# Eight fp32 products of a zeroed tile on TensorE around the two modulation products of a transformer block

## The chip, the core and the metric

The kernel runs on one core of one Trainium2 chip. Its time is the device time of one execution in microseconds (us); lower is better. The engines are named as in the profile: PE is TensorE's matmul (PEld its weight load), DVE is VectorE, ACT is ScalarE, POOL is GpSimd, SP is SyncE, which issues most DMAs.

## What is computed

One conditioned transformer block on x of 32 sequences x 32 tokens x 256, all in fp32: an RMS norm whose scale comes from a product of the conditioning vector with a 256 x 256 matrix, attention with 8 query heads and one key and value head of 32 columns with rotary positions, a residual, a second RMS norm with a scale of its own, and a gated MLP of 1024.

```python
def ada_rms(x, t, w, tw):
    n = x * jax.lax.rsqrt(jnp.mean(jnp.square(x), axis=-1, keepdims=True) + EPS)
    scale = t @ tw.T
    return n * (w * (1.0 + scale))[:, None, :]
h = ada_rms(x, time_emb, ln1_w, ln1_tw)
q, k, v = heads(h @ Wq.T), heads(h @ Wk.T), heads(h @ Wv.T)
q = apply_rope(q, pos_ids)
k = apply_rope(k, pos_ids)
scores = jnp.einsum('bkgsd,bktd->bkgst', qg, k) / jnp.sqrt(jnp.float32(HD))
attn = jax.nn.softmax(scores, axis=-1)
x = res + ctx @ Wo.T
h = ada_rms(x, time_emb, ln2_w, ln2_tw)
mlp = jax.nn.silu(h @ Wg.T) * (h @ Wu.T) @ Wd.T
return res + mlp
```

(`heads` stands here for the reshapes.)

## The kernel before

The 1024 tokens are eight tiles of 128, taken two at a time as four groups, g = 0 to 3. Each engine has a program of its own, written out by hand in the order in which the engine runs it, and the programs meet only at semaphores. So the order on PE is that of the calls at the end of its block, and a product that PE has not yet come to holds up everything behind it.

PE begins with `norm_scale(0)` (L274 in the profile: four products of 128x32 into the bank `ps_s`, once `pa`, the pack with the conditioning and the first matrix, has landed). DVE turns them into the modulation `mod` (L454) and multiplies it into the transposed input, `hx` (L251). ACT rounds that to `hx_h` (L805), DVE or POOL takes the remainder `hx_l` (L256), and `qkv` (L293) forms the projections from three rounded products (high by high, low by high, high by low). The weights are split in the same way: `wqkv_h` on ACT (L868, L870) and `wqkv_l` on POOL (L977). Before the second tile's attention PE does `norm_scale(1)` (L274 into `ps_t`, once `pb` has landed), the modulation of the second norm. Then the first attention follows tile by tile: `scores` (L305), the maxima `top` (L574) and differences `below` (L583) on DVE, the exponential on ACT, `turn_probs` (L316), `context` (L330) and `project` (L340). All products that are not of the rounded kind, L274, L305, L330 and L340 among them, are plain fp32: each of them is two MATMULs in the trace. The rotation of queries and keys on DVE (`rot_b` L526, `rot_a` L533, `qkT` L556, `kbd` L562) needs tables that are made from the norm's factor.

From some 31 us on PE runs the gate and up products of the MLP (`gate_up`, L367) of one group, with the attention of the next group and the down products (L262 to L264) between them. The down products accumulate in two banks, of which `ps_d` is one; before that `ps_d` holds the projections of `qkv(1, 0)`, `qkv(2, 0)` and `qkv(3, 0)`, each of which begins by overwriting it.

Of the kernel before, what the change touches and what calls it, by code (L numbers as in the profile page):

```python
# [14 lines left out]
P = 128  # L15
BATCH, SEQ, HIDDEN = 32, 32, 256
# [39 lines left out]
def block_program(nc, xT, x_tok, pos, pack_s, pack_a, w_qkv, pack_b, w_gu, w_d, out):  # L56
    with ExitStack() as ctx:
        def sb(name, shape, dt=F32):
            return ctx.enter_context(nc.sbuf_tensor(name, shape, dt))

        def sem(name):
            return ctx.enter_context(nc.semaphore(name))
# [32 lines left out]
        sin = sb("sin", [P, 2, TILES, HALF])  # L95
        mod = [sb(f"mod{n}", [P, KH, BATCH]) for n in range(2)]
        half_neg = sb("half_neg", [P, CT])


        hx = sb("hx", [P, GROUPS, KH, GT])  # L100
# [39 lines left out]
        ps_d = ctx.enter_context(nc.psum_tensor("ps_d", [P, CT, HIDDEN], F32))  # L140
# [8 lines left out]
        out_done = sem("out_done")  # L149

        chain = sem("chain")
        half_ready = sem("half_ready")
        sin_ready = sem("sin_ready")
        mod_ps = sem("mod_ps")
        mod_ready = [sem(f"mod_ready{n}") for n in range(2)]
# [57 lines left out]
        def done(g, c, n):  # L213
            return g * CT + c + n

        def span(c, n, width):
            return slice(c * width, (c + n) * width)


        def bank_s(g, c, n):  # L220
            return ps_gu[:, 0].rearrange("p u t -> p (u t)") if (g, c) == (0, 1) else ps_s[:, :]
# [10 lines left out]
        def bank_qkv(g, c):  # L232

            if g == 0:
                return ps_a[:, c, 0:QKV]
            return (ps_d[:, :, :].rearrange("p c n -> p (c n)"),
                    ps_gu[:, RING - 1].rearrange("p u t -> p (u t)"))[c][:, 0:QKV]
# [29 lines left out]
        def _(pe):  # L267
            def norm_scale(n):

                w, loaded, bank = ((tw1, in_pa, ps_s), (tw2, in_pb, ps_t))[n]  # L270
                pe.wait_ge(loaded, 16)
                for f in range(KH):
                    for k in range(KH):
                        mm = pe.matmul(bank[:, span(f, 1, BATCH)], w[:, k, span(f, 1, P)], cond[:, k, :],  # L274
                                       start=(k == 0), stop=(k == KH - 1))
                mm.then_inc(mod_ps, 1)

            def qkv(g, c):


                if g > 1:
                    pe.wait_ge(qkv_copied, CT * (g - 2) + c + 1)
                maker, before = (0, 0) if g == 0 else (1, CT)
                pe.wait_ge(hx_hi, done(g, c, 1))
                for step, (x, w) in enumerate(((hx_h, wqkv_h), (hx_l, wqkv_h), (hx_h, wqkv_l))):
                    if step == 1:
                        pe.wait_ge(hx_lo[maker], done(g, c, 1) - before)
                    for k in range(KH):
                        if g == 0 and step == 0:
                            pe.wait_ge(wqkv_hi, k + 1)  # L290
                        if g == 0 and step == 2:
                            pe.wait_ge(wqkv_lo, k + 1)
                        mm = pe.matmul(bank_qkv(g, c), x[:, g, k, span(c, 1, P)], w[:, k, :],  # L293
                                       start=(step == 0 and k == 0), stop=(step == 2 and k == KH - 1))
                mm.then_inc(qkv_ready, 1)

            def scores(g, c0, n):
                if g == 0:
                    pe.wait_ge(mod_ready[0], 1)
                else:  # L300
                    pe.wait_ge(x2_ready, CT * g)
                pe.wait_ge(kbd_ready, done(g, c0, n))
                for c in range(c0, c0 + n):
                    for j in range(HG):
                        mm = pe.matmul(bank_s(g, c0, n)[:, span(c * HG + j, 1, P)], qkT[:, c, span(j, 1, P)],  # L305
                                       kbd[:, c].rearrange("p b t -> p (b t)"), start=True, stop=True)
                mm.then_inc(scores_ready, n)
# [75 lines left out]
                    mm.then_inc(down_ready, 1)  # L383


            norm_scale(0)
            qkv(0, 0)
            qkv(0, 1)
            norm_scale(1)
            scores(0, 0, 1)  # L390
            qkv(1, 0)
            turn_probs(0, 0, 1)
# [46 lines left out]
        def _(dve):  # L439
            steps = [0]  # L440

            def link(ins):
# [2 lines left out]
                ins.then_inc(chain, 1)  # L445
                dve.wait_ge(chain, steps[0])

            dve.memset(half_neg[:, :], -0.5).then_inc(half_ready, 1)

            def modulation():  # L450
# [598 lines left out]
```

## Time and profile before

| | us |
|---|---|
| three timed runs | 122.69, 124.89, 126.38 |
| median | 124.89 |
| span of the profiled execution, first to last instruction | 121.7 |
| PE busy in it | 104.9 (86%) |
| DVE busy | 86.7 (71%) |
| POOL busy | 53.5 |
| ACT busy | 53.0 |

Of the profiled execution only the span is recorded, not a device time of its own around it. The fastest timed run is 1.0 us above the span and the median 3.2 us. The three runs lie 3.7 us apart. In the timeline each row gives the start in us, the duration in us of all its instructions together, engine, line, operation, what is written and read, the shapes, the count, and in brackets the idle time of the engine before the row with what ended it. The durations of MATMULs overlap, so where one follows another the distance of their starts is the time that one takes.

### The profile page before, as it was taken

Reading aid. Unit: us, or ns where it says so; the run is one execution under the profiler, and the core shown is the slowest. Engines: PE = TensorE matmul, PEld = TensorE weight load, DVE = VectorE, ACT = ScalarE, POOL = GpSimd, SP = SyncE. Lnnn points to the kernel's source line nnn. Section 1 sums busy time; section 2 is a strip of 40 time slices with the busy share of each in tenths; the row PEclk is TensorE's granted clock in tenths of the full one; section 3 lists DMA queues with packets and bytes.
Section 4 is the critical chain, followed back from the end, with each engine's and each line's share of the span. In section 5 each row is a group of like instructions: output and inputs, shape, how many; then the busy total and the mean of one; then the engine's idle time right before and its main releaser. Section 6 shows DMA issues by size and latency. Waiting matters only on the chain.

```text
span 121.7 us, 2393 instructions
## 1 busy us (share of the span) xinstructions
PE 104.9 (86%) x768; PEld 100.5 (83%) x768; DVE 86.7 (71%) x207; ACT 53.0 (44%) x140; POOL 53.5 (44%) x59
## 2 busy tenths in 40 slices
PE   0658487983977999979999999999999999999991
PEld 0548366863867999969999999999999999999990
DVE  0587985789999976986889598688947453756411
ACT  4083578651951493143137624224562422455300
POOL 0065787756399429734033543402344231244610
PEclk9999869999687699999999999999999999999999
DMA  3999995000000000000000200000020000020011
GB/s 93 241 296 416 424 422 229 7 3 0 5 0 0 0 3 0 5 0 0 0 5 0 86 3 0 5 0 0 0 86 5 0 3 0 16 78 0 3 37 54
DMA packets 3421, 7.69 MB, mean 63 GB/s; under 512 B 592, under 2 KB 1616, under 8 KB 3408
## 3 DMA queue, kind: packets, MB, share of 16 engines
q1 hardware_dynamic: 3120, 7.25, 16.3%
q10 hardware_dynamic: 288, 0.27, 1.1%
q8 instruction: 7, 0.11, 0.4%
q14 instruction: 6, 0.05, 0.2%
HBM read 6.47 MB, written 1.05 MB: 62 GB/s over the span
## 4 chain that ended last, share of the span: by engine, by line
PE 63%; DVE 19%; issue 6%; DMA 4%; ACT 3%; POOL 1%; SPq 1%; DVEq 0%; POOLq 0%
PE ps_gu L367 34%; DVE kbd L562 4%; DMA wqkv<-in_w_qkv 4%; PE ps_s L305 4%; PE ps_a L264 3%; PE ps_a L262 3%; PE ps_a L263 3%; PE ps_d L262 3%; PE ps_d L263 3%; PE ps_d L264 3%; PE ps_a L330 2%; DVE rot_b L526 2%; DVE qkT L556 1%; PE ps_t L340 1%; PE ps_s L340 1%
## 5 line engine op out<-in xcount | busy, mean ns | idle before, releaser
L953 POOL TENSOR_TENSOR hf_l<-hf,hf_h 128x256 fp32r<-128x256 f32 x32 | 24.3, 758 | 45.5 <-ACT hf_h L853 45.5
L367 PE MATMUL ps_gu<-h_h,wgu_h 128*128 128x256 f32 x128 | 28.1, 302 | 0.2 <-ACT h_h L825 0.2
L367 PE MATMUL ps_gu<-h_h,wgu_l 128*128 128x256 f32 x128 | 26.6, 291 | 0.0
L367 PE MATMUL ps_gu<-h_l,wgu_h 128*128 128x256 f32 x128 | 26.6, 290 | 0.0
L846 ACT ACTIVATE th<-ps_gu 128x256 f32<-128x256 f32 x32 | 12.2, 382 | 24.9 <-PE ps_gu L367 24.8
L853 ACT ACTIVATE hf_h<-hf 128x256 fp32r<-128x256 f32 x32 | 13.2, 412 | 20.0 <-DVE hf L657 20.0
L367 PEld LDWEIGHTS ps_gu<-h_h,wgu_h 128*128 128x128 f32 x128 | 21.0, 200 | 0.6 <-ACT h_h L825 0.4
L648 DVE SCALAR_TENSOR_TENSOR sg<-th,ps_gu 128x256 f32<-128x256 f32 x32 | 13.3, 417 | 11.2 <-ACT th L846 10.8
L367 PEld LDWEIGHTS ps_gu<-h_l,wgu_h 128*128 128x128 f32 x128 | 20.8, 199 | 0.0
L367 PEld LDWEIGHTS ps_gu<-h_h,wgu_l 128*128 128x128 f32 x128 | 20.7, 199 | 0.0
L657 DVE TENSOR_TENSOR hf<-sg,ps_gu 128x256 f32<-128x256 f32 x32 | 13.4, 418 | 0.8
L966 POOL TENSOR_TENSOR wgu_l<-wgu,wgu_h 128x1024 fp32r<-128x1024 f32 x4 | 9.5, 2388 | 4.3 <-ACT wgu_h L857 4.3
L262 PE MATMUL ps_d<-wd_h,hf_h 128*128 128x256 f32 x32 | 9.1, 286 | 0.9 <-POOL hf_l L953 0.9
L262 PE MATMUL ps_a<-wd_h,hf_h 128*128 128x256 f32 x32 | 9.3, 290 | 0.0
L263 PE MATMUL ps_d<-wd_l,hf_h 128*128 128x256 f32 x32 | 9.1, 283 | 0.0
L264 PE MATMUL ps_a<-wd_h,hf_l 128*128 128x256 f32 x32 | 9.0, 282 | 0.0
L263 PE MATMUL ps_a<-wd_l,hf_h 128*128 128x256 f32 x32 | 9.0, 281 | 0.0
L264 PE MATMUL ps_d<-wd_h,hf_l 128*128 128x256 f32 x32 | 9.0, 281 | 0.0
L305 PE MATMUL ps_s<-kbd,qkT 128*128 128x128 f32 x28 | 4.7, 316 | 3.6 <-DVE kbd L562 3.6
L305 PEld LDWEIGHTS ps_s<-kbd,qkT 128*128 128x128 f32 x28 | 4.0, 218 | 3.8 <-issue 3.8
L262 PEld LDWEIGHTS ps_d<-wd_h,hf_h 128*128 128x128 f32 x32 | 6.0, 188 | 1.2 <-issue 1.1
L562 DVE TENSOR_TENSOR kbd<-qkT,small 128x128 f32<-128x128 f32 (+1 forms) x6 | 6.2, 1038 | 0.3
(117 smaller groups left out, 208.4 us busy)
## 6 DMA issues: line engine op xcount, KB each, us to landing
wgu<-in_w_gu SPq DMA_DIRECT2D x4, 512.0 KB, 10.4
wd<-in_w_d SPq DMA_DIRECT2D x2, 512.0 KB, 12.6
xk<-in_x_tok SPq DMA_DIRECT2D x1, 768.0 KB, 10.1
out_x<-xk SPq DMA_DIRECT2D x3, 256.0 KB, 2.2
pb<-in_pack_b SPq DMA_DIRECT2D x1, 576.0 KB, 8.5
xt<-in_xT SPq DMA_DIRECT2D x1, 512.0 KB, 9.2
wqkv<-in_w_qkv SPq DMA_DIRECT2D x1, 320.0 KB, 5.0
pa<-in_pack_a SPq DMA_DIRECT2D x1, 288.0 KB, 3.1
```

The costliest lines, as they stand in the source:

```text
L262: pe.matmul(ps, lhs_h, rhs_h, start=first, stop=False)
L263: pe.matmul(ps, lhs_h, rhs_l, start=False, stop=False)
L264: return pe.matmul(ps, lhs_l, rhs_h, start=False, stop=last)
L305: mm = pe.matmul(bank_s(g, c0, n)[:, span(c * HG + j, 1, P)], qkT[:, c, span(j, 1, P)], kbd[:, c].rearrange("p b t -> p (b t)"), start=Tru ...
L367: mm = pe.matmul(ps_gu[:, n % RING, part, :], w[:, m, span(part * KH + k, 1, P)], h[:, k, :], start=(step == 0 and k == 0), stop=(step == ...
L562: dve.tensor_tensor(kbd[:, cs, :, :], qkT[:, cs, HEADS * HD:QK].unsqueeze(2).broadcast_to([P, n, BPT, SEQ]), mask.unsqueeze(1).unsqueeze(3 ...
L648: dve.scalar_tensor_tensor(out=sg[:, n % RING], in0=th[:, n % RING], scalar=1.0, in1=ps_gu[:, n % RING, 0, :], op0=ALU.add, op1=ALU.mult). ...
L657: dve.tensor_tensor(hf[:, m], sg[:, n % RING], ps_gu[:, n % RING, 1, :], ALU.mult).then_inc(hf_ready, 1)
L846: act.activation(th[:, n % RING], ps_gu[:, n % RING, 0, :], ACT.Tanh, scale=0.5).then_inc(th_ready, 1)
L853: act.activation(hf_h[:, m], hf[:, m], ACT.Copy).then_inc(hf_hi, 1)
L953: pool.tensor_tensor(hf_l[:, m], hf[:, m], hf_h[:, m].bitcast(F32), ALU.subtract).then_inc(hf_lo, 1)
L966: pool.tensor_tensor(wgu_l[:, sl, :], wgu[:, sl, :], wgu_h[:, sl, :].bitcast(F32), ALU.subtract).then_inc(wgu_lo, 1)
```

## The change

A tile `blank` of 128 x 256 is set to zero by DVE as its first instruction. A new semaphore, `blank_ready`, is waited for by PE ahead of its first product. PE then multiplies `blank` with itself, 128 weight columns by 256 moving columns in plain fp32, into the first half of `ps_d`: four products ahead of `norm_scale(0)`, two behind it and two behind `norm_scale(1)`. Each product starts a sum of its own, and nothing reads the result; `qkv(1, 0)` overwrites the bank later. No other engine waits for these products.

```diff
+        blank = sb("blank", [P, HIDDEN])
...
+            def warm(n):
+
+                for _ in range(n):
+                    pe.matmul(ps_d[:, 0, :], blank[:, 0:P], blank[:, :], start=True, stop=True)
+
+            pe.wait_ge(blank_ready, 1)
+            warm(4)
             norm_scale(0)
+            warm(2)
             qkv(0, 0)
             qkv(0, 1)
             norm_scale(1)
+            warm(2)
             scores(0, 0, 1)
...
+            dve.memset(blank[:, :], 0.0).then_inc(blank_ready, 1)
             dve.memset(half_neg[:, :], -0.5).then_inc(half_ready, 1)
```

The start of PE's program before (a row's count is of products, not of MATMULs):

```order
0 L266 UNCONDITIONAL_BRANCH
1 L274 MATMUL ps_s<-pa 128x32 x4
2 L293 MATMUL ps_a<-wqkv_h,hx_h 128x320 x2
3 L293 MATMUL ps_a<-wqkv_h,hx_l 128x320 x2
4 L293 MATMUL ps_a<-wqkv_l,hx_h 128x320 x2
5 L293 MATMUL ps_a<-wqkv_h,hx_h 128x320 x2
6 L293 MATMUL ps_a<-wqkv_h,hx_l 128x320 x2
7 L293 MATMUL ps_a<-wqkv_l,hx_h 128x320 x2
8 L274 MATMUL ps_t<-pa,pb 128x32 x4
9 L305 MATMUL ps_s<-kbd,qkT 128x128 x2
```

The same stretch of PE's program now, where the new lines push the line numbers on by one (L390 is the new product):

```order
0 L267 UNCONDITIONAL_BRANCH
1 L390 MATMUL ps_d<-blank 128x256 x4
2 L275 MATMUL ps_s<-pa 128x32 x4
3 L390 MATMUL ps_d<-blank 128x256 x2
4 L294 MATMUL ps_a<-wqkv_h,hx_h 128x320 x2
...
9 L294 MATMUL ps_a<-wqkv_l,hx_h 128x320 x2
10 L275 MATMUL ps_t<-pa,pb 128x32 x4
11 L390 MATMUL ps_d<-blank 128x256 x2
12 L306 MATMUL ps_s<-kbd,qkT 128x128 x2
```

The three groups of new products stand ahead of the first modulation, between it and the first projection, and between the second modulation and the first scores; nothing else moved.

The start of DVE's program now:

```order
1 L458 MEMSET blank 128x256
2 L459 MEMSET half_neg 128x2
3 L493 TENSOR_TENSOR ang<-pos_sb,small 128x128
4 L495 TENSOR_SCALAR redu<-ang 128x128
5 L496 TENSOR_SCALAR turns<-redu 128x128
```

Only the first row is new; the others follow as before.

## Rows read from the trace of the kernel before

**Rows 1.** The page: chain that ended last, by engine and by line.

```profile
PE 63%; DVE 19%; issue 6%; DMA 4%; ACT 3%; POOL 1%; SPq 1%; DVEq 0%; POOLq 0%
PE ps_gu L367 34%; DVE kbd L562 4%; DMA wqkv<-in_w_qkv 4%; PE ps_s L305 4%; PE ps_a L264 3%; PE ps_a L262 3%; PE ps_a L263 3%; PE ps_d L262 3%; PE ps_d L263 3%; PE ps_d L264 3%; PE ps_a L330 2%; DVE rot_b L526 2%; DVE qkT L556 1%; PE ps_t L340 1%; PE ps_s L340 1%
```

**Rows 2.** Timeline, 0 to 12 us: first modulation, first projections, second modulation.

```profile
0.80 0.06 DVE L448 MEMSET half_neg<- 128x2 f32 x1 [0.80 <-PEq L1038]
...
3.86 1.92 PE L274 MATMUL ps_s<-pa 128*128 128x32 f32 x8 [3.86 <-DMA pa<-in_pack_a]
...
5.95 0.41 DVE L454 TENSOR_SCALAR mod<-ps_s,small 128x32 f32<-128x32 f32 x2
6.39 0.76 DVE L251 TENSOR_TENSOR hx<-xt,mod 128x256 f32<-128x256 f32 x2
6.71 0.47 ACT L868 ACTIVATE wqkv_h<-wqkv 128x320 fp32r<-128x320 f32 x1 [0.25 <-DMA wqkv<-in_w_qkv]
...
7.08 0.40 ACT L805 ACTIVATE hx_h<-hx 128x256 fp32r<-128x256 f32 x1
7.26 1.86 POOL L977 TENSOR_TENSOR wqkv_l<-wqkv,wqkv_h 128x320 fp32r<-128x320 f32 x2 [6.82 <-ACT wqkv_h L868]
...
7.54 0.99 PE L293 MATMUL ps_a<-wqkv_h,hx_h 128*128 128x320 f32 x2 [1.76 <-ACT hx_h L805]
...
8.32 0.95 DVE L476 SCALAR_TENSOR_TENSOR redu<-sin_in 128x128 f32<-128x128 f32 x1
...
11.56 1.08 PE L274 MATMUL ps_t<-pa,pb 128*128 128x32 f32 x8 [0.33 <-DMA pb<-in_pack_b]
...
11.83 0.52 DVE L526 TENSOR_TENSOR rot_b<-ps_a,sin_r 128x144 f32<-128x144 f32 x2
```

**Rows 3.** Timeline, 14 to 19 us: scores of the first and the second tile.

```profile
14.41 1.19 PE L305 MATMUL ps_s<-kbd,qkT 128*128 128x128 f32 x4 [1.77 <-DVE kbd L562]
...
15.63 0.42 DVE L574 TENSOR_REDUCE top<-ps_s 128x8 f32<-128x256 f32 x1 [0.58 <-PE ps_s L305]
...
17.02 0.69 PE L316 MATMUL ps_t<-pb,prob 128*128 128x128 f32 x2
...
18.14 0.68 PE L305 MATMUL ps_gu<-kbd,qkT 128*128 128x128 f32 x4 [0.43 <-DVE kbd L562]
```

**Rows 4.** Short stretches: busy per engine, granted clock, DMA share, GB/s.

```profile
14.10:14.20 0.10, 0.00 (x0) 0.00 (x0) 0.10 (x2) 0.00 (x0) 0.10 (x2) 0.94 1.03 430
14.20:14.30 0.10, 0.00 (x0) 0.00 (x0) 0.10 (x2) 0.09 (x1) 0.10 (x1) 0.50 1.23 512
17.50:17.60 0.10, 0.10 (x2) 0.00 (x0) 0.10 (x2) 0.10 (x1) 0.10 (x1) 0.50 0.90 369
17.60:17.70 0.10, 0.10 (x1) 0.00 (x0) 0.10 (x2) 0.07 (x1) 0.10 (x1) 1.00 0.99 410
```

**Rows 5.** Longer stretches; busy of PE, PEld, DVE, ACT, POOL; clock; DMA.

```profile
10.78:14.19 3.41, 1.52 (x11) 1.15 (x10) 3.27 (x10) 1.27 (x3) 2.00 (x3) 1.00 1.02 420
14.19:17.60 3.41, 3.19 (x12) 2.71 (x12) 2.76 (x10) 2.70 (x4) 3.41 (x3) 0.50 1.02 420
17.60:21.01 3.41, 2.57 (x17) 1.99 (x16) 2.29 (x8) 2.92 (x7) 2.10 (x2) 1.00 0.69 280
...
27.84:31.25 3.41, 1.60 (x10) 1.33 (x11) 3.29 (x6) 0.75 (x3) 1.44 (x1) 1.00 0.02 5
...
34.66:38.07 3.41, 1.62 (x14) 1.44 (x14) 3.38 (x5) 1.33 (x2) 3.41 (x3) 1.00 0.00 0
38.07:41.48 3.41, 3.41 (x19) 3.41 (x18) 3.35 (x5) 0.89 (x3) 2.21 (x3) 0.50 0.00 0
41.48:44.89 3.41, 3.41 (x31) 3.41 (x31) 2.58 (x7) 2.79 (x10) 1.38 (x2) 1.00 0.01 2
```

**Rows 6.** Timeline of PE, 49 to 51 us: projections of 128x256 in fp32.

```profile
49.75 1.02 PE L340 MATMUL ps_s<-pb,ctxT 128*128 128x256 f32 x4
50.61 1.03 PE L340 MATMUL ps_t<-pb,ctxT 128*128 128x256 f32 x4
```

More of the change, by code:

```diff
@@ L151, in block_program @@
         chain = sem("chain")
-        half_ready = sem("half_ready")
+        half_ready, blank_ready = sem("half_ready"), sem("blank_ready")
         sin_ready = sem("sin_ready")
```

## The prediction

> **What bounds the kernel now.** I read the chain of waits by engine first, to see who sets the end, then the timeline of the first 19 us, where the change lies, and last the granted clock in stretches. By the chain PE makes 63% of the span, and over half of that is the gate and up products [rows 1], which start at 31 us. The change touches nothing there. What it can do to the end is to bring the first attention, and with it everything behind it, earlier or later. So the question is what sets the pace from 0 to 19 us. In the timeline PE stands still until `pa` lands at 3.86, then again until 7.54, and waits 1.77 us before the scores at 14.41 and 0.43 us before those at 18.14 [rows 2, 3]: in that part it is mostly waiting for DVE, and a faster PE gains only where somebody waits for it. The one place of size is DVE's maximum at 15.63, which stood idle 0.58 us for the first scores [rows 3].
>
> The clock is the other reading. The granted clock falls to 0.50 (1.2 GHz) at 14.2 us and is back at 1.00 (2.4 GHz) at 17.6 [rows 4]. Before its first change the record says 1.00, but the durations do not bear it out: the eight MATMULs of the first modulation took 1.92 us, the same eight of the second 1.08 us [rows 2]. I take it that PE ran at the low level from the start until it had worked through the first projections. Behind each fall PE had been little busy: 1.52, 1.60 and 1.62 us in the 3.41 us ahead of 14.19, 31.25 and 38.07; in the stretch from 17.60, after which it kept 1.00, it was busy 2.57 us [rows 5].
>
> **The price of one product.** Two fp32 products of 128x256 are four MATMULs, and from the first of one set to the first of the next it is 50.61 - 49.75 = 0.86 us, so 0.43 us a product at 2.4 GHz [rows 6]. No row has them at 1.2 GHz. The scores went from 0.68 to 1.19 us between the levels [rows 3], a factor of 1.75, and twice is the most: 0.75 to 0.86 us a product, of which I take 0.86, since nothing but the array works on 256 columns.
>
> **The memset and the four products ahead of the first modulation.** The memset takes DVE's first place at 0.80 us. The trace has a memset of 128x2 with 0.06 us and an operation of 128x256 with 0.38 us (0.76 for two) [rows 2]: 0.06 to 0.38, and I take 0.3, near the upper end since the size is the same. On DVE it costs nothing, whose next work comes behind the DMA of the positions after 4 us. PE starts at 1.15 us and, at the low level, works 4 x 0.86 = 3.44 us, until 4.6. `pa` is there at 3.86, so the modulation starts 0.74 us later. If it also stays slow it ends at 6.5 and not at 5.78; DVE, which was ready for it only at 5.95, writes `mod` some 0.6 us later. From there: `hx` at 7.0, its first half done at 7.4, where ACT wanted it at 7.08, so 0.3 us late. The next cover is POOL: `wqkv_l` runs to 7.26 + 1.86 = 9.12 whatever `hx` does, and DVE's `redu` at 8.32 took 0.95 us although `hx`, twice as large, took 0.38 a piece, so it was held until POOL was through. The 0.3 us go into that stall, and the path to the tables and `rot_b` at 11.83 stays, or slips by up to 0.15 us by ACT's second half of `wqkv_h`, which stands behind `hx_h` in its queue. If the clock comes up within the four products, the modulation takes 1.08 us in place of 1.92 and even this is gone (4.3 + 1.1 = 5.4, before 5.78). I take 0 for this part, and -0.1 to +0.7 as bounds: the upper end is the whole delay without cover.
>
> **The two products behind it.** They stand before the first projection, which waits for `hx_h` until 7.54 [rows 2]. From 5.4 they end at 6.3 at the high level, from 6.5 at 8.2 at the low one. The second delays the first projection by 0.7 us. Its reader is `rot_b` at 11.83, which waits for the tables, and the two projections were through before the second modulation at 11.56 in spite of the low level; at the high level they would be done earlier. So 0 on the path; only `norm_scale(1)`, which waits for `pb` until 11.56, would start up to 0.3 us later.
>
> **The two products behind the second modulation.** It begins at 11.56 and ends at 12.64 at the high level. Two products end at 13.5, or at 14.35 if they are slow. The scores wait for `kbd` until 14.41 [rows 3], so both fit, the slow ones just. What they do is to fill the gap that stood before the fall at 14.19: PE's busy time there goes from 1.52 to 1.52 + 0.86 = 2.38 us. That is nearer to the 2.57 us of the stretch after which it kept the clock than to 1.62 us [rows 5]. If it is kept, the first scores take 0.68 us and not 1.19: 0.51 us earlier, less than the 0.58 us for which DVE idled, so DVE passes all of it on. `turn_probs` at 17.02 goes from 0.69 to some 0.69 / 1.75 = 0.4, on ACT's side, with nobody waiting who is on the path. The projections between them are hidden behind POOL's `hx_l` and DVE. So **-0.51 us**.
>
> **What is late next, and whether it lasts.** Behind the scores DVE, ACT and POOL follow one another by semaphores, and no DMA landing stands in the way: the DMA share is 1.02 up to 17.60, 0.69 to 21.01 and 0.00 from 27.84 [rows 5]. The chain shifts as a whole to the first group of the loop, where PE takes over. I find no place that gives it back for certain.
>
> **The sum.** 0 + 0 - 0.51 = -0.5 us, against the profiled execution 121.7 - 0.5 = 121.2 us of span. The same step on the median is 124.89 - 0.5 = **124.4 us**. The profiled execution lies 3.2 us under the median, and the three runs are 3.7 us apart, so the clock or something else differs from run to run by more than the whole gain. Within 2%, which is 2.5 us, a measurement of this kernel tells little from no change.
>
> The Trainium skill, page "TensorE: Matmul & The Clock Gate", Part 1, says that the default state is the throttled one and activity releases it, and adds for modelling that "the ramp penalty is <1% of a typical kernel span". By that rule no warm-up can give over 1.2 us here; my rows price it at 0.5, which agrees. The same page's table of what to do says that the clock falls back after an idle gap between bursts. This trace fell at 14.19 with 1.52 us of work before it, and no gap of PE there is over 1.8 us; the row decides.
>
> **The rivals.**
>
> First, **nothing arrives** (124.9 us): the clock is no better at 14.2 us, since the projections at the high level are themselves shorter, and PE, which then waits for POOL's `wqkv_l`, is less busy from 7.5 to 10.8. Then it falls before the second modulation, the last two products run slow and end at 13.5 + 1.7 = 15.2 us at worst, in front of the scores. Against a scores start of 14.41 this is +0.8 us, from which a clock that comes up meanwhile gives back 0.5 or more. For it: the low level is where PE's work fills its time. Against: 2.4 us of work in place of 1.5.
>
> Second, the one on the **slower side**: the fall is put off, not removed. With fast scores and projections PE is less busy between 14.2 and 17.6 than the 3.19 us that it had at the low level [rows 5]: 0.68 for the scores, 1.6 / 1.75 = 0.9 for what filled 15.4 to 17.02, and 0.4, some 2.0 us of work. If it falls at 17.6, the second tile is slow up to 21 us: scores +0.51, turning the probabilities +0.3, and the context products, which are four MATMULs of nearly the scores' size, +0.5, all on the chain: +1.3 - 0.5 = +0.8, so 125.7 us. It decides if those 2.0 us of work act like the 1.6 us ahead of a fall and not like the 2.57 us of the stretch that kept its clock; they lie halfway, and here a run of the clock's changes at other moments can turn it. It is slower, yet not by 2%; it would need another low stretch in the loop beside it, +1.3 us (below), to reach 127.4.
>
> Third, **more than the scores**: with the chain 0.5 us earlier, PE arrives earlier at the loop too and the fall at 38.07 does not come. In the low stretch from there PE did 19 MATMULs, in the next one of the same length 31 [rows 5], and it was on the path: 3.41 x (1 - 19/31) = 1.3 us. The time would be 124.4 - 1.3 = 123.1 us. For more than 2% a further 0.7 us would be needed, as from a run whose first attention was slow throughout.
>
> Fourth, **the first modulation's delay has no cover**: +0.7 - 0.5 = +0.2, 125.1 us.
>
> **How the numbers follow.** The forecast has 0.42; nothing arrives 0.22; put off 0.12; more than the scores 0.14; delay without cover 0.10. All of these lie between 123.1 and 125.7. The median itself moves by about 0.9 us with the luck of the runs (half of the mean distance from 124.89 to its neighbours, 1.5 and 2.2 us), which gives 122.2 to 126.6; since the upper cases hold less chance I end it at 126.2. Faster by over 2% (under 122.4) takes the third rival and luck: 0.11. Slower by over 2% (over 127.4) takes the second and bad luck: 0.06. Within 2%: 0.83.
>
> **What would show it.** In the profile of the changed kernel: PE's new products begin at about 1.15 us and take 3.0 to 3.5 us; the first modulation's eight MATMULs take 1.1 us and not 1.9; `redu` still ends at about 9.3 us and `rot_b` still starts at about 11.8; the granted clock is 1.00 at 14.4 and the first scores take about 0.7 us; DVE's maximum starts at about 15.1. I am wrong if `rot_b` starts over 0.3 us later, if the clock shows 0.50 between 14 and 21 us, or if the end moves by more than the start of the loop does.

## The result

| | executions | median us | lowest to highest |
|---|---|---|---|
| changed kernel | 4 | 124.66 | 124.37 to 127.39 |
| kernel before, the same session | 4 | 125.63 | 122.69 to 127.26 |

The ratio of the changed kernel to the one before was given as 1.019, 95% interval 1.0126 to 1.0253: slower, although its median is the lower one. The ratio counts only executions within 1.5% of the fastest of their kernel, which of these eight leaves the one of 122.69 us against three with a mean of 124.56 us, or 1.015, so the 1.019 cannot be worked out from them. The profiled execution of the changed kernel has a span of 122.6 us, 0.9 more than before, and took 124.37 us as a whole.

Later sessions ran both kernels again. Over all of them the changed kernel has 22 executions with a mean of 124.6 us (standard deviation 1.7) and the kernel before 76 with a mean of 124.8 us (1.7; two of 254 and 257 us left out). The difference is -0.1 us with a standard error of 0.4; with each of the three sessions that ran both compared by itself it is -0.5 +- 0.5 us. So **the eight products made no difference that could be measured**. The forecast of -0.5 us lies within the error, and so does zero; the 0.9 us more of the first comparison of spans lies over two errors away, so I take the first ratio for chance.

The page of the changed kernel, chain by engine and by line:

```profile
PE 68%; DVE 17%; issue 6%; DMA 3%; ACT 3%; POOL 0%; SPq 0%; DVEq 0%
PE ps_gu L368 33%; DVE kbd L573 4%; PE ps_s L306 4%; PE ps_a L294 3%; DMA pos_sb<-in_pos 3%; PE ps_a L264 3%; PE ps_a L265 3%; PE ps_a L263 3%; PE ps_d L263 3%; PE ps_d L264 3%; PE ps_d L265 3%; PE ps_a L331 2%; PE ps_d L390 2%; PE ps_s L341 1%; PE ps_t L341 1%
```

Against [rows 1] the first link is another: the chain starts at the DMA of the positions, `pos_sb`, and no longer at the weights, and the new products (L390) hold 2% of it. The timeline of the same stretch as [rows 2] and [rows 3]:

```profile
0.86 0.27 DVE L458 MEMSET blank<- 128x256 f32 x1 [0.86 <-PEq L1049]
...
1.19 3.66 PE L390 MATMUL ps_d<-blank 128*128 128x256 f32 x8 [1.19 <-DVE blank L458]
...
4.68 0.97 PE L275 MATMUL ps_s<-pa 128*128 128x32 f32 x8
5.06 0.29 DVE L493 TENSOR_TENSOR ang<-pos_sb,small 128x128 f32<-128x128 int32 x1 [3.92 <-DMA pos_sb<-in_pos]
...
5.49 1.11 PE L390 MATMUL ps_d<-blank 128*128 128x256 f32 x4
...
6.82 0.41 DVE L465 TENSOR_SCALAR mod<-ps_s,small 128x32 f32<-128x32 f32 x2
...
9.03 0.95 DVE L487 SCALAR_TENSOR_TENSOR redu<-sin_in 128x128 f32<-128x128 f32 x1
...
12.53 0.52 DVE L537 TENSOR_TENSOR rot_b<-ps_a,sin_r 128x144 f32<-128x144 f32 x2
...
13.55 2.05 PE L390 MATMUL ps_d<-blank 128*128 128x256 f32 x4
...
15.40 1.19 PE L306 MATMUL ps_s<-kbd,qkT 128*128 128x128 f32 x4
...
18.90 0.68 PE L306 MATMUL ps_gu<-kbd,qkT 128*128 128x128 f32 x4 [0.36 <-DVE kbd L573]
```

The start went as priced: the memset 0.27 us, the four products 1.19 to 4.68 us, the first modulation's eight MATMULs 0.97 us. But `mod` is at 6.82 us and not at 5.95, and PE has no part in that: its product was through at 5.65. DVE was not ready, because it makes the angles before the modulation and could start them only at 5.06 us, once the positions had landed. In the kernel before it could at 4.19 us:

```profile
4.19 0.29 DVE L482 TENSOR_TENSOR ang<-pos_sb,small 128x128 f32<-128x128 int32 x1 [3.32 <-DMA pos_sb<-in_pos]
```

That 0.87 us is still there at `rot_b` (12.53 against 11.83, +0.70), at the second scores (+0.76) and at the end (+0.9). The granted clock of the changed kernel, one stretch a line (busy of PE, PEld, DVE, ACT, POOL, then clock, DMA share, GB/s), answers [rows 5]:

```profile
4.59:8.00 3.41, 2.01 (x13) 1.53 (x12) 2.70 (x11) 1.14 (x4) 0.23 (x1) 1.00 0.91 251
8.00:11.41 3.41, 3.22 (x10) 2.83 (x11) 2.72 (x8) 1.91 (x8) 2.77 (x4) 0.50 0.98 392
11.41:14.83 3.42, 3.42 (x14) 3.24 (x14) 3.28 (x9) 1.68 (x4) 3.02 (x3) 0.50 1.03 425
14.83:18.24 3.41, 3.41 (x13) 2.70 (x13) 2.76 (x8) 1.83 (x4) 2.55 (x3) 0.50 1.02 419
18.24:21.65 3.41, 2.76 (x18) 2.04 (x17) 2.42 (x9) 3.07 (x7) 1.66 (x1) 1.00 0.52 214
```

That the first line reads 1.00 does not tell when the clock came up, since the record reads 1.00 from the start. By the durations it was by some 4.6 us: the four products took 3.49 us, start to start, which is 0.87 each and the price of the low level, and the modulation behind them 0.97 us, where it took 1.92 in the kernel before. The clock fell at 8.0 us and stayed at 1.2 GHz for 10.2 us, over both projections, the second modulation, the two blank products behind it and the first scores. So the products behind the second modulation did not hold the clock: they ran at 1.2 GHz themselves. In the kernel before, the last of the first projections is the first to be quick, so there the clock came up at some 10.8 us, and it fell at 14.2 [rows 4]. Rise and fall both came some 6 us earlier in the changed kernel.

```profile
10.22 0.71 PE L293 MATMUL ps_a<-wqkv_h,hx_l 128*128 128x320 f32 x2
10.75 0.48 PE L293 MATMUL ps_a<-wqkv_l,hx_h 128*128 128x320 f32 x2
```

### The profile page after: what moved, and what is told of

It is laid out like the page before. It is cut to its first block, busy times and chain, and to the rows that moved or that the text cites. A ratio compares the mean times of both kernels' runs of the same rounds, so it can differ in the third digit from the quotient of the medians.

```text
span 122.6 us, 2426 instructions
## 1 busy us (share of the span) xinstructions
PE 110.7 (90%) x784; PEld 105.1 (86%) x784; DVE 87.2 (71%) x208; ACT 52.8 (43%) x140; POOL 53.5 (44%) x59
## 4 chain that ended last, share of the span: by engine, by line
PE 68%; DVE 17%; issue 6%; DMA 3%; ACT 3%; POOL 0%; SPq 0%; DVEq 0%
PE ps_gu L368 33%; DVE kbd L573 4%; PE ps_s L306 4%; PE ps_a L294 3%; DMA pos_sb<-in_pos 3%; PE ps_a L264 3%; PE ps_a L265 3%; PE ps_a L263 3%; PE ps_d L263 3%; PE ps_d L264 3%; PE ps_d L265 3%; PE ps_a L331 2%; PE ps_d L390 2%; PE ps_s L341 1%; PE ps_t L341 1%
## 5 line engine op out<-in xcount | busy, mean ns | idle before, releaser
L659 DVE SCALAR_TENSOR_TENSOR sg<-th,ps_gu 128x256 f32<-128x256 f32 x32 | 13.4, 417 | 11.1 <-ACT th L857 10.8
L390 PE MATMUL ps_d<-blank 128*128 128x256 f32 x16 | 6.8, 587 | 1.2 <-DVE blank L458 1.2
## 6 DMA issues: line engine op xcount, KB each, us to landing
xk<-in_x_tok SPq DMA_DIRECT2D x1, 768.0 KB, 10.2
```

What stands on the lines that cost most here:

```text
L659: dve.scalar_tensor_tensor(out=sg[:, n % RING], in0=th[:, n % RING], scalar=1.0, in1=ps_gu[:, n % RING, 0, :], op0=ALU.add, op1=ALU.mult). ...
```

## The experiments

Two theories. **A:** the difference is chance, made by things that vary from run to run in both kernels (where the positions land, what VectorE meets on GpSimd, when the clock changes), and the eight products are worth a few tenths at most. **B:** the products cost the 0.9 us that the two first profiles show between them.

### Both kernels again, and each half of the change

No edit in `before_again` and `after_again`.

> The kernel before, unchanged, against itself. Theory A (the changed kernel's 0.9 us more of span is chance: the positions' DMA landed 0.87 us later, and that varies from run to run): the first angle operation on VectorE starts anywhere from 4.2 to 5.1 us here too, the span is 121.7 to 122.7 us, and the timed runs spread over 3 us or more, ratio 1.00 with an interval of about 0.01. Theory B (the products cost it): the first angle operation starts at 4.2 us as in the first profile, the span is within 0.3 us of 121.7.

> The changed kernel, unchanged. Theory A (chance): ratio 0.99 to 1.01, the interval holding 1.00, and the first angle operation need not start at 5.06 us again. Theory B (the products cost 0.9 us or more): ratio 1.007 to 1.02, the first angle operation again at about 5.06 us, the second rotation product again late.

The third keeps `warm(4)` alone, the fourth only the `warm(2)` behind `norm_scale(1)`:

```diff
             warm(4)
             norm_scale(0)
-            warm(2)
             qkv(0, 0)
             qkv(0, 1)
             norm_scale(1)
-            warm(2)
```

> Only the four products ahead of the first modulation (and the memset). Theory B, that these four delay the start: the modulation at 6.8 us, rotation at 12.5, span 122.4, ratio 1.005 or more. Theory A: the angle operation and not the modulation product sets the modulation's time, and the ratio is 1.00 within 0.007. On the clock: the granted clock rises at about 4 to 5 us and falls before 12 us, so that the second modulation's eight products take 1.1 or 1.9 us, depending on the run.

> Only the two products behind the second modulation. If the products there delay the scores (the part of the 0.9 us that is not the late DMA, 0.1 to 0.3 us): the scores follow the last blank product at once when these run at the low clock, start about 0.1 to 0.3 us behind the key tile, ratio 1.00 to 1.003. If they hold the clock up as forecast: first scores 0.68 us in place of 1.19, span 121.2, ratio 0.996. The two differ in the clock over 14 to 18 us: 0.50 or 1.00.

Six executions each: `before_again` median 124.69 us, ratio 1.0005 (0.9916 to 1.0093); `after_again` 124.48; `first_four_only` 125.17, 0.9983 (0.9783 to 1.0184); `last_two_only` 124.93, 1.0081 (0.9972 to 1.019). The session's executions of the kernel before had a median of 125.76. Nothing stands out. The unchanged kernel's second profile, timeline from the start:

```profile
3.67 1.92 PE L274 MATMUL ps_s<-pa 128*128 128x32 f32 x8 [3.67 <-DMA pa<-in_pack_a]
5.36 0.29 DVE L482 TENSOR_TENSOR ang<-pos_sb,small 128x128 f32<-128x128 int32 x1 [4.49 <-DMA pos_sb<-in_pos]
7.12 0.41 DVE L454 TENSOR_SCALAR mod<-ps_s,small 128x32 f32<-128x32 f32 x2
...
16.15 1.19 PE L305 MATMUL ps_s<-kbd,qkT 128*128 128x128 f32 x4 [3.06 <-DVE kbd L562]
```

The angles start at 5.36 us without any new product, later than in the changed kernel. **The 0.87 us was the landing of the positions, and that varies by itself**: the angles start at 4.19 and 5.36 in the kernel before, at 5.06, 5.02 and 5.58 in the changed one. Theory B loses its ground in the profile here, and the means above speak against its 0.9 us. Yet this run's span is 121.2 us, the lower of the two, since its second group met a better clock. From 35.75 us it was granted 1.00 where [rows 5] has 0.50 from 38.07 on:

```profile
35.75:39.16 3.41, 3.41 (x29) 3.28 (x29) 3.41 (x3) 2.24 (x4) 3.41 (x2) 1.00 0.00 0
```

`last_two_only` shows the half that the forecast rested on. Its second modulation took 1.75 us, the blank products 2.05, and both scores had the durations of 1.2 GHz after all:

```profile
12.45 1.75 PE L275 MATMUL ps_t<-pa,pb 128*128 128x32 f32 x8
14.01 2.05 PE L390 MATMUL ps_d<-blank 128*128 128x256 f32 x4
14.96 0.52 DVE L535 TENSOR_TENSOR rot_b<-ps_a,sin_r 128x144 f32<-128x144 f32 x2
...
18.32 1.20 PE L306 MATMUL ps_s<-kbd,qkT 128*128 128x128 f32 x4 [2.26 <-DVE kbd L571]
...
21.84 1.19 PE L306 MATMUL ps_gu<-kbd,qkT 128*128 128x128 f32 x4 [0.20 <-DVE kbd L571]
```

They did not delay the scores either, which waited 2.26 us for the key tile. This run does not repeat the forecast's case, though: by the durations its clock had not come up at all before them, where the forecast had it up from 10.8 us.

### The positions first; eight products in place of four; products before the loop

```diff
+            sp.dma_start(pos_sb[:, :], pos).then_inc(in_pos, 16)
             sp.dma_start(pa[:, :], pack_a).then_inc(in_pa, 16)
-            sp.dma_start(pos_sb[:, :], pos).then_inc(in_pos, 16)
```

> The kernel before with the DMA of the positions issued first on its queue, ahead of the pack of the first modulation. Theory A (the start of the angles, at 4.2 to 5.5 us in six profiles, is set by where the positions land behind the pack, and that is the scatter at the start): the first angle operation starts at 3.3 to 3.8 us in both kernels of this pair, the modulation is then set by its product, and the span falls by 0.5 to 1.0 us against a late-landing run, ratio 0.993 to 0.998. Rival (the landing is late whatever stands ahead, as the path of many small pieces): the angles still start at 4.2 to 5.5 us and the ratio is 1.00.

> The changed kernel with the positions' DMA first in the same way. If the four products ahead of the first modulation are free only because the angles are late, then now they show: TensorE reaches the modulation product at 4.7 us where the pack has landed at about 4.2, the modulation is written at 5.9 to 6.2 us, later by up to 0.4 us than in the pair's other kernel if that comes at the low clock's 1.9 us anyway (4.2 + 1.9 = 6.1) it is the same. Theory A: ratio to the pair's other kernel 1.00 within 0.007.

Medians 125.56 and 125.09 us (ratios 0.9987, 0.9901 to 1.0073, and 0.9952, 0.9869 to 1.0036). The angles start at 2.80 and 2.61 us, but now the pack lands late, at 5.58 and 5.51 us in place of 3.7 to 3.9. Here the four products do what they can do: in the kernel without them the first modulation's product takes 1.92 us and `mod` is written at 7.61, with them it takes 1.08 us and `mod` comes at 6.70, 0.9 us earlier. By `rot_b` (13.03 against 12.41) 0.6 us of it is left, and by the first scores (16.01 against 16.06) nothing. So the change of order, expected to give 0.993 to 0.998, moved the late landing from one DMA to the other.

In `eight_ahead` `warm(8)` stands in place of `warm(4)`:

> The changed kernel with eight products ahead of the first modulation in place of four. They end at about 1.2 + 3.4 + 4 x 0.43 to 0.86 = 6.3 to 8 us, behind the angles, so now they must delay the modulation: written at 7.3 to 9 us. Theory A (four cost nothing since the angles are later): ratio 1.005 to 1.02 here. Theory B (four cost 0.9 us already): another 1.5 to 3 us on top, ratio 1.02 to 1.035.

Median 125.22 us, ratio 1.0223 (1.0119 to 1.0327), in a session where the kernel before had a median of 124.70. That is just inside the range of theory B, but the means are 125.2 against 124.5 us, +0.7 +- 0.4 us, which decides for neither theory. The profile does: the products ran from 1.18 to 7.41 us, the modulation was written from 8.49 on, and DVE waited 1.40 us for it. So ahead of the modulation four products are covered by the late positions, and eight are not.

In `gap_before_loop` all eight are gone, and four stand in the loop's first group:

```diff
                 gate_up(g, 1)
+                if g == 0:
+                    pe.wait_ge(blank_ready, 1)
+                    pe.wait_ge(qkv_copied, TILES - CT)
+                    warm(4)
                 scores(a, 0, CT)
```

> None of the eight products of the change; four of them instead in the loop's first group, between the second gate and up product and the scores, where TensorE waits 1.8 us for the key tile. If the clock stretch at 38 us is what costs (1.3 us by the rows of the kernel before): the granted clock stays 1.00 from about 35 us on, the low stretch from 38 to 41.5 us is gone, span 120.4 us from a start like the first profile's, ratio about 0.990. If the clock does not follow what TensorE does there: low stretch as before, ratio 1.00 or above by the 1.7 us that the four products take at most.

PE waits there for the copies of the projections too, which share the bank `ps_d`. Median 125.06 us, ratio 1.0145 (0.9992 to 1.0298), where 0.990 was expected. The clock did stay at 1.00 from 37.03 us on, yet `before_again` and `before_pos_first` had no low stretch there either, so one profile shows nothing about cause. The products began at 38.81 us and the scores at 40.53, while the key tile was ready at 39.34 (36.89 + 2.45): they stood in front of the scores for 1.1 us. Inconclusive on the clock.

### What VectorE meets on GpSimd

In this profile, and in `last_two_only` and `eight_ahead`, the rotation product came 2 us later than in the others. Timeline of `gap_before_loop`:

```profile
11.54 2.05 POOL L252 TENSOR_TENSOR hx<-xt,mod 128x512 f32<-128x512 f32 x2
11.68 0.99 DVE L511 TENSOR_TENSOR cos_r<-cos,rstd 128x64 f32<-128x64 f32 x1 [0.66 <-POOL rstd L952]
12.59 1.08 DVE L514 TENSOR_TENSOR sin_r<-sin,rstd 128x64 f32<-128x64 f32 x1
...
13.55 1.26 POOL L257 TENSOR_TENSOR hx_l<-hx,hx_h 128x512 fp32r<-128x512 f32 x1
13.59 1.24 DVE L516 TENSOR_TENSOR mask_r<-small,rstd 128x8 f32<-128x8 f32 x1
14.87 0.52 DVE L537 TENSOR_TENSOR rot_b<-ps_a,sin_r 128x144 f32<-128x144 f32 x2
```

An operation on 128x8 elements takes 1.24 us: each of the three table operations ends with an operation of GpSimd. Where the third input piece lands a little later, GpSimd pauses between its operations, DVE gets through, and `mask_r` takes 0.15 us. So it was in the kernel before, where GpSimd stood idle from 11.50 to 12.91 us and `sin_r` and `mask_r` (11.50 to 11.79) fell into the pause:

```profile
10.46 1.04 POOL L251 TENSOR_TENSOR hx<-xt,mod 128x512 f32<-128x512 f32 x1
...
12.91 1.20 POOL L251 TENSOR_TENSOR hx<-xt,mod 128x512 f32<-128x512 f32 x1 [1.41 <-DMA xt<-in_xT]
```

So a delay of a few tenths ahead of this place can become 2 us, or nothing. The same hold decides whether the second group's key tiles take 2.47 + 1.96 us, as in the kernel before, or 0.28 + 0.29 us, as in `before_pos_first`. The Trainium skill, page "SBUF — State Buffer", section "SBUF: two separate sides", says that VectorE and GpSimd take a shared pair of ports as an exclusive lock held for the whole instruction, that an operation of VectorE with two inputs in SBUF needs it against one of GpSimd that reads SBUF, and that the loser is blocked. The rows above, of such operations on both engines, agree: 1.24 us in place of 0.15.

```diff
             pool.wait_ge(mod_ready[0], 1)
+            pool.wait_ge(tab_ready, 1)
             modulate_x(1)
...
+            pool.wait_ge(xn_ready, CT)
             low_gu(1)
+            pool.wait_ge(kbd_ready, 2 * CT)
             low_gu(2)
```

The first wait alone, without and with the eight products:

> The kernel before, with one wait more on GpSimd: the modulation of the second group's input comes behind the rotation tables. Theory A (the scatter at the start is VectorE held while GpSimd runs a long operation: in the profiles so far the three table operations took 1.2 to 3.2 us in all, depending on whether the third input piece had landed): the tables take 0.6 us (0.20 + 0.21 + 0.16) in every profile, the first rotation product starts 0.8 us or more earlier against the angles, and the span falls by 0.5 to 2.5 us, ratio 0.985 to 0.997. Rival (the hold only moves to the next operations of VectorE): tables 0.6 us, but the key tile no earlier, ratio 1.00.

> The changed kernel with the same wait on GpSimd. The pair (this against the kernel before with the tables first) shows the eight products with less scatter. If the products are worth nothing: both ratios to the kernel before are within 0.006 of each other. If they hold the clock for the first scores, as forecast: 0.5 us, so 0.004 lower. If they cost 0.9 us, as the first comparison read: 0.007 higher, with the two slow products behind the second modulation in front of the scores.

The first and the third:

> As the kernel before with the tables first, and besides GpSimd takes the remainder of the third quarter of the gate and up weights only once the second group's key tiles are made. Theory A: the two key tile operations, 2.47 + 1.96 us in the first profile and 0.28 + 0.29 us in the kernel with the positions first, take 0.28 us each every time, the scores of the second group start 1.5 us or more earlier, the span is about 119 to 120 us, ratio 0.975 to 0.99. Rival: the later weights then hold TensorE at the fifth gate and up product, and the gain is given back, ratio 0.995 to 1.00.

All three, without and with the eight products:

> The kernel before with three waits on GpSimd: its modulation behind the rotation tables, the remainder of the second quarter of the gate and up weights behind the scaled second tile of the first group, that of the third quarter behind the second group's key tiles. Theory A (VectorE held during GpSimd's long operations is the largest waste before the loop): the scaling that took 2.42 us takes 0.3 us, the loop's first gate and up product starts at 28.5 to 30.5 us in place of 31 to 33, ratio 0.965 to 0.98. Rival (the later weights hold TensorE): ratio 0.98 to 0.99, no better than with two waits.

> The changed kernel with the same three waits. No effect of the eight products: ratio within 0.006 of the pair's other kernel. Forecast's mechanism (clock kept up for the first scores): 0.004 lower, scores 0.68 us. Cost of 0.9 us as in the first comparison: 0.007 higher. On the clock I expect a rise within or right behind the first four products, a fall at 8 to 10 us, and no pattern after that which differs from the pair's other kernel.

And the changed kernel once more:

> The changed kernel a third time, for the mean of its executions and one more profile. Theory A (no effect): mean within 0.8 us of the kernel before's executions in the same session. Theory B (products cost 0.9 us): mean 0.9 us or more above. In the profile: the angles start anywhere from 4.2 to 5.5 us, the clock has risen by 4 to 7 us, and falls again at least once before the second scores.

| kernel | executions | mean us | ratio to before, interval |
|---|---|---|---|
| tables first | 12 | 124.8 | 0.9954, 0.9882 to 1.0027 |
| the same with the eight products | 6 | 123.2 | none given |
| tables and keys first | 6 | 122.5 | 0.9838, 0.9778 to 0.9898 |
| three waits | 6 | 122.1 | 0.9893, 0.9777 to 1.0009 |
| three waits with the eight products | 6 | 121.0 | 0.9843, 0.9750 to 0.9937 |
| changed kernel, third time | 12 | 124.4 | 0.9921, 0.9846 to 0.9997 |

The executions of the kernel before had means of 125.0 us in the session of the first, second, third and last line and of 123.9 us in that of the other two. With the tables first the three operations took 0.23, 0.22 and 0.16 us, and yet that wait alone gave nothing that could be measured: its interval holds 1.00, and its mean is 0.2 +- 0.8 us below the kernel before. With the keys first as well both key tiles took 0.28 and 0.29 us, the span was 119.1 us, and the mean is 2.5 +- 0.8 us below. In `before_three_waits` the wait that was new, behind the scaled tile, gained nothing that shows: the scaling took 0.35 us, but the next operation was held in its place, and the first gate and up product came at 32.12 us, against 31.38 with two waits and 28.5 to 30.5 expected. The rival had the ratio right, not the reason; no row that I read shows late weights holding TensorE. The rows of `before_three_waits`:

```profile
28.06 0.35 DVE L623 TENSOR_SCALAR xn<-xk,rstd 128x256 f32<-128x256 f32 x1 [0.21 <-POOL rstd L947]
...
28.49 2.51 POOL L966 TENSOR_TENSOR wgu_l<-wgu,wgu_h 128x1024 fp32r<-128x1024 f32 x1 [0.47 <-DVE xn L623]
...
28.69 2.59 DVE L639 TENSOR_TENSOR h_l<-h,h_h 128x256 fp32r<-128x256 f32 x1
```

The version with three waits and the eight products is the fastest here: median 121.01 us, against 123.92 for the kernel before in its session. Two waits and the products together were not run.

### What the eight products are worth

The pairs that differ only in the products, as differences of mean times (one execution of 254.9 us left out with the positions first): -0.1 +- 0.4 us (plain), -0.7 +- 0.8 (positions first), -1.6 +- 0.9 (tables first), -1.1 +- 0.5 (three waits). Weighted by their errors that is -0.6 +- 0.3 us. All four point down, only one by over twice its error; the third holds an execution of 131.2 us on the side without the products, and without it is -1.0 +- 0.7. The profiles do not bear the means out: in three of the four pairs the spans with the products are the longer ones (122.6, 122.7 and 123.4 against 121.7 and 121.2 us; 120.8 against 120.1; 123.1 against 119.2; 118.4 against 119.8). A gain of 0 to 1.2 us is possible and not shown.

If there is one, the scores are where the profiles let it come from. The scores' four MATMULs took 0.68 us at the high clock and 1.19 at the low one. Means over the profiles, eight without products ahead of the modulation (before, before_again, before_pos_first, gap_before_loop, last_two_only, before_tables_first, before_tables_and_keys_first, before_three_waits) and eight with them:

| | first scores us | second scores us |
|---|---|---|
| without | 1.19 1.19 0.85 1.19 1.20 0.68 1.20 1.19, mean 1.09 | 0.68 1.19 0.89 1.19 1.19 0.68 0.68 1.20, mean 0.96 |
| with | 1.19 0.93 1.19 1.20 1.19 0.68 1.06 1.19, mean 1.08 | 0.68 0.86 0.68 0.68 0.68 0.73 0.68 1.19, mean 0.77 |

(The second line is after, after_again, after_third, first_four_only, after_pos_first, after_tables_first, after_three_waits, eight_ahead.) The first scores are the same. The second ones are shorter by 0.2 us, and what stands near them follows: in the three-waits pair DVE waited 2.38 us for the second context without the products and 1.36 with them, and from the first scores to the second `xn` it was 14.10 us there and 12.33 with the products. Eight against eight with this scatter, over kernels that differ in more than the products, is a hint, no more.

What quick first scores give is as the forecast said. In `after_tables_first` they took 0.68 us, and DVE had its maximum 0.72 us behind their start, against 1.22 in the kernel before (14.41 and 15.63, [rows 3]):

```profile
15.23 0.68 PE L306 MATMUL ps_s<-kbd,qkT 128*128 128x128 f32 x4 [0.63 <-DVE kbd L573]
...
15.95 0.43 DVE L585 TENSOR_REDUCE top<-ps_s 128x8 f32<-128x256 f32 x1
```

But `before_tables_first` has 0.68 us there too, without any product.

**What no profile here shows.** The profiled spans lie between 118.4 and 123.9 us, but other executions reach 127.0 us. The granted clock does not sort them: over 72 executions of the kernel before the correlation of span and mean clock is 0.01, and the thirteen with a mean clock of 0.986 or 0.987 run from 120.2 to 127.0 us (the mean clock counts the start, where the record reads 1.00, as quick). So the three causes found below 124 us need not be those of the long executions; what these are stays open.

## Why the prediction was wrong, point by point

- **What bounds the start.** Right that PE is mostly waiting. Wrong in taking as given that DVE is ready for the modulation at 5.95 us. That hangs on the angles, which start at 4.19 us in one draw of a DMA, and started anywhere from 4.07 us (`before_three_waits`) to 5.75 us (`after_tables_first`) behind it. That term was missing from the sum and its scatter is larger than the sum.
- **The memset and four products.** Right: 0.27 us, 3.5 us, `mod` not delayed by them. The cover was the late positions, more than POOL's `wqkv_l`; doubling the products used it up. But they bring the clock up early, and that undid the step of the last two products.
- **The two behind the first modulation.** Right, nothing waits for them.
- **The two behind the second modulation, -0.51 us.** This is the step that failed. It left the fall at 14.2 us where it was and asked only whether PE was busy enough ahead of it, though the four products in front were to bring the rise forward. In the changed kernel the clock had come up by 4.6 us and was down from 8.0 to 18.24, before these products began, and the first scores took 1.19 us and not 0.68: 0 in place of -0.51 us. They gained nothing in the means either (1.09 against 1.08 us). The other profiles bear this out. With four products in front the first fall on record comes at 7.9 to 9.3 us in six of seven, and at 12.4 us in the seventh (`after_three_waits`); in the eight profiles with none in front it never comes before 14.2 us, and comes as late as 34.4 (`last_two_only`). With eight in front, in one profile, it came at 16.9 us, which stays unexplained. That quick scores would be passed on by DVE was right, as `after_tables_first` showed. The size of the sum, -0.5, may still be near the truth (-0.6 +- 0.3, not shown), by the second scores: then it was right by luck.
- **The rivals.** The first came closest: the clock fell before the second modulation and the last two products ran slow, 13.55 us to the scores' start at 15.40, where the key tile was ready at 15.25. The scores start as far behind the key tile in the kernel before (14.26 and 14.41), so they cost nothing there; in `after_three_waits`, where the key tile was ready at 14.11 and the scores came at 14.44, they cost 0.2 us. The second's mechanism, a fall that is put off, did show (`after_tables_first` granted 0.50 again after 19.5 us). The third's, a low stretch that does not come, was real but had nothing to do with the products: `before_again` had none behind 35.75 us either, and the changed kernel had one from 38.7 to 42.1 us.
- **The range** of 122.2 to 126.2 held the measured median of 124.66 us. What it got wrong was the direction of the first comparison, 1.019, which the later sessions do not bear out. The spread of 3.7 us in three runs was noted and should have been read as the main fact. The 3.2 us between the profiled execution and the median are no such spread: they set a span against a time, and on record a time is 1.7 us or more longer than its own span, mostly 1.8.
- **Its own signs of being wrong.** Two of three showed: `rot_b` started 0.70 us later, where over 0.3 was the mark, and the clock read 0.50 between 14 and 21 us. The first of them was the positions, not the products. The third did not: the loop's first gate and up product was 0.94 us later (31.91 against 30.97) and the end 0.9.

## What to carry to other kernels

Before costing a change of 0.5 us from one profile, ask which starting times in it are draws: a small DMA behind a large one, the moments at which the clock changes, and short VectorE operations that last until a GpSimd operation ends. Here the profiled spans of kernels that differed in nothing but blank products went from 121.2 to 123.9 us, and those three are what was found to differ between them. Taking away the third at the tables and key tiles by two waits on GpSimd gave 1.6%, in one session, where warming TensorE gave nothing that could be measured in the kernel as it was. Blank products are free only in front of a wait that is longer than they are, and the clock that they bring up need not stay: here it was up by 4.6 us and down again at 8.0, with PE busy 2.01 of the 3.41 us between.

## What was not expected of the hardware

- The clock fell at 8.00 us although PE had been busy 2.01 of the 3.41 us before, and stayed low over 3.22 and 3.42 us of nearly full work, some of it blank products and products of 32 columns; it came back at 18.24 after 3.41 us more.
- Ahead of the first change on record the granted clock reads 1.00 while the durations are those of 1.2 GHz: in `last_two_only` the second scores at 21.84 us took 1.19 us, and the stretch around them reads 1.00:

```profile
20.00:24.00 4.00, 3.80 (x17) 3.20 (x16) 2.32 (x8) 2.70 (x5) 0.92 (x1) 1.00 0.07 27
```

- A DMA of 4 KB issued behind one of 288 KB landed for its reader at 4.07 to 5.75 us from run to run; issued ahead of it, the angles could start at 2.61 and 2.80 us, and the large one was read at 5.51 and 5.58 us, 1.7 us later.
- An operation of 128x8 elements on VectorE took 0.15 us (`before`) or 1.25 us (`last_two_only`), as GpSimd was idle or busy.
